# Second layer's matrix scaled by rows on VectorE, the last sums in two banks, an early exponential, and the weighing one slot sooner

## The reference

```python
x = _layernorm(x + L0(x, adj))        # (adj @ x + x) @ W + b, divided by its own length
x = _layernorm(x + L1(x, adj))        # 5 steps of a gated recurrent unit; each multiplies by adj
x = _layernorm(x + L2(x, adj))
x = _layernorm(x + L3(x, adj))

# L2
A_hat = adj + eye
d = sum(A_hat, axis=-1) ** (-0.5)
A_norm = d[:, None] * A_hat * d[None, :]
out = (A_norm @ x) @ W.T + b
# L3
A = softmax(where(adj > 0, e[cumsum(adj > 0) - 1], NEG), axis=1)
out = (A * eye) @ (x @ W0) + (A * (1 - eye)) @ (x @ W1) + bias
```

## Time and profile before

| | |
|---|---|
| median of 3 runs | 771.02 us (769.65 to 773.0) |
| the profiled execution | 769.01 us |
| its span, first to last instruction | 767.1 us |
| busy: PE, DVE, ACT, POOL | 98%, 81%, 67%, 22% |
| granted TensorE clock | 0.998 |
| moved by DMA | 16.60 MB |

### The profile page before, as it was taken

How to read it: one execution, slowest core, us unless ns; L and a number is a source line. 1 busy time by engine, 2 the same in 40 slices (tenths; PEclk the granted TensorE clock), 3 DMA queues, 4 the chain that set the end, 5 groups by cost and what they waited for, 6 DMA issues and landing times.

```text
span 767.1 us, 11992 instructions
## 1 busy us (share of the span) xinstructions
PE 751.2 (98%) x3788; PEld 630.1 (82%) x3788; DVE 624.6 (81%) x1447; ACT 513.7 (67%) x1072; POOL 166.2 (22%) x314
## 2 busy tenths in 40 slices
PE   8999999999999999999999999999999999899996
PEld 7888788888888888888888888888887887789885
DVE  5899998888888788877777777887999998785663
ACT  4799877666667766666666666666587857875444
POOL 1778420000000000000000000000123257764334
PEclk9999999999999999999999999999999999999999
DMA  7500000000030001000000000000000000000112
GB/s 226 204 1 2 1 1 1 1 1 1 0 117 1 1 1 56 1 0 1 1 1 0 0 0 0 0 0 2 1 1 1 1 1 1 3 14 28 56 56 83
DMA packets 9895, 16.60 MB, mean 22 GB/s; under 512 B 2929, under 2 KB 4465, under 8 KB 9201
## 3 DMA queue, kind: packets, MB, share of 16 engines
q1 hardware_dynamic: 9840, 15.94, 6.1%
HBM read 8.59 MB, written 5.24 MB: 18 GB/s over the span
## 4 chain that ended last, share of the span: by engine, by line
PE 78%; DVE 9%; ACT 7%; POOL 2%; issue 2%; DMA 1%; SPq 0%; DVEq 0%; ACTq 0%
PE agg_ps L971 12%; PE agg_ps L973 12%; PE agg_ps L972 12%; PE gate_ps L907 7%; PE gate_ps L909 6%; PE gate_ps L908 6%; PE cand_ps L907 4%; PE cand_ps L909 4%; PE cand_ps L908 4%; PE turn_ps L1010 4%; PE gate_ps L914 2%; PE cand_ps L914 2%; DVE stats L810 2%; ACT res L428 2%; ACT feat L505 1%
## 5 line engine op out<-in xcount | busy, mean ns | idle before, releaser
L971 PE MATMUL agg_ps<-adj_hi,nat_hi 128*128 128x512 f32 x384 | 152.1, 396 | 0.0
L973 PE MATMUL agg_ps<-adj_hi,nat_lo 128*128 128x512 f32 x384 | 150.1, 391 | 0.0
L972 PE MATMUL agg_ps<-adj_lo,nat_hi 128*128 128x512 f32 x384 | 149.6, 390 | 0.0
L629 POOL TENSOR_SCALAR shift<-mean_var 128x4 f32<-128x4 f32 x64 | 25.6, 400 | 427.1 <-DVE mean_var L814 424.8
L767 DVE TENSOR_TENSOR agg_lo<-agg_ps,agg_hi 128x512 fp32r<-128x512 f32 x80 | 55.2, 690 | 65.0 <-ACT agg_hi L457 65.0
L490 ACT ACTIVATE reset_hi<-gate_r 128x512 fp32r<-128x512 f32 x80 | 50.6, 633 | 83.1 <-DVE gate_r L784 83.1
L973 PEld LDWEIGHTS agg_ps<-adj_hi,nat_lo 128*128 128x128 f32 x384 | 72.1, 188 | 16.2
L972 PEld LDWEIGHTS agg_ps<-adj_lo,nat_hi 128*128 128x128 f32 x384 | 72.2, 188 | 15.6
L971 PEld LDWEIGHTS agg_ps<-adj_hi,nat_hi 128*128 128x128 f32 x384 | 72.1, 188 | 15.4 <-DVE adj_lo L833 0.3
L474 ACT ACTIVATE gate_r<-gate_ps,bias 128x512 f32<-128x512 f32 x80 | 55.2, 690 | 43.5 <-PE gate_ps L909 43.5
L457 ACT ACTIVATE agg_hi<-agg_ps 128x512 fp32r<-128x512 f32 x80 | 48.7, 608 | 45.3 <-PE agg_ps L973 45.3
(11 more groups left out here) (181 smaller groups left out, 1794.2 us busy)
## 6 DMA issues: line engine op xcount, KB each, us to landing
res<-in_x SPq DMA_DIRECT2D x16, 256.0 KB, 5.3
out<-res SPq DMA_DIRECT2D x16, 256.0 KB, 2.0
rows<-in_adj SPq DMA_DIRECT2D x4, 256.0 KB, 4.0
adj_hi<-eye_hi SPq DMA_DIRECT2D x1, 1024.0 KB, 9.6
adj_lo<-eye_lo SPq DMA_DIRECT2D x1, 1024.0 KB, 11.5
later<-in_adj SPq DMA_DIRECT2D x1, 1024.0 KB, 6.5
mix_rows<-mix SPq DMA_DIRECT2D x1, 1024.0 KB, 8.0
later<-mix_rows SPq DMA_DIRECT2D x1, 1024.0 KB, 4.9
```

Of the source, the lines that this page charges most:

```text
L971: pe.matmul(ps, nat_hi[:, b, k, :], m_hi[:, k, :], start=(k == 0), stop=False)
L972: pe.matmul(ps, nat_hi[:, b, k, :], m_lo[:, k, :], start=False, stop=False)
L973: last = pe.matmul(ps, nat_lo[:, b, k, :], m_hi[:, k, :], start=False, stop=(k == T - 1))
```

## The change

Four edits are made.

1. L2's matrix is no longer transposed on TensorE. `adj_hi + adj_lo` is the transposed `adj`, so DVE adds the two into `later` and adds the identity to the block's own 128 columns (slots 39 to 42, `WHOLE_AT`), and multiplies each block by `d_cols`, the row of all scales (slots 42 to 45). ACT and DVE make `eye_hi` and `eye_lo` from `later`. The row comes by two DMAs: `row_d` to DRAM, then back spread over all partitions. The four turns "l2", the scaling of rows on ACT and `diag_d` go.
2. For unit 127 the sums lie in two banks, two quarters in each; TensorE reports each half. DVE takes statistics of the first half after the first report. DVE adds the epsilon itself, subtracts the mean while POOL takes the power, and ends with one multiplication of 512 columns. For unit 126, DVE also takes the epsilon and the negated mean from POOL.
3. ACT takes one exponential of one column, `warm`, at the end of slot 100.
4. The reciprocal and the diagonal's multiplication move to the head of DVE's slot 106, and the weighing (ACT and DVE) from slot 107 to the end of slot 106.

```diff
-SCALE_AT = SUM_AT + 3
-L2_AT = SCALE_AT + 3
+WHOLE_AT = SUM_AT + 2
+L2_AT = WHOLE_AT + T
 assert L2_AT + T < LOOP_FROM
 
 EXP_AT = AFTER + 6
 INV_AT = EXP_AT + T
-WEIGH_AT = INV_AT + 1
-MIX_AT = WEIGH_AT + 1
+MIX_AT = INV_AT + 2
...
+        def last_sums():
+
+            one, two = layer_ps[(UNITS - 1) % 4], agg_ps[UNITS % 2]
+            return [ps[:, :].rearrange("p (t d) -> p t d", t=T)[:, part, :] for ps, part in zip((one, two), HALVES)]
...
+            sp.wait_ge(row_d_made, 1)
+            sp.dma_start(d_dram[0].rearrange("(t p) -> p t", p=P), row_d[:, :],
+                         allow_slow_non_contiguous=True).then_inc(d_stored, 16)
+            sp.wait_ge(d_stored, 16)
+            sp.wait_ge(turned, TURN_NO["value", T - 1] + 1)
+            sp.dma_start(d_cols[:, :], d_dram[0:1, :].to_broadcast([P, N])).then_inc(d_cols_in, 16)
             sp.wait_ge(mix_stored, 16)
-            sp.wait_ge(turn_read, reads(TURN_NO["l2", T - 1]))
+            sp.wait_ge(l2_lo_made, T)
...
-                for k in range(2 * (s - SCALE_AT), 2 * (s - SCALE_AT) + 2):
-                    if 0 <= k < T:
-                        act.wait_ge(rows_again, 16)
-                        act.wait_ge(row_d_made, 1)
-                        act.activation(later[:, k, :], later[:, k, :], ACT.Copy,
-                                       scale=row_d[:, k:k + 1]).then_inc(rows_scaled, 1)
                 k = s - L2_AT
                 if 0 <= k < T:
                     act.wait_ge(mix_stored, 16)
-                    n = TURN_NO["l2", k]
-                    act.wait_ge(turned, n + 1)
-                    act.activation(eye_hi[:, k, :], turn_ps[n % 2][:, :], ACT.Copy,
+                    act.wait_ge(l2_scaled, k + 1)
+                    act.activation(eye_hi[:, k, :], later[:, k, :], ACT.Copy,
                                    scale=row_d[:, k:k + 1]).then_inc(l2_hi_made, 1)
+                if s == EXP_AT - 2:
+
+                    act.wait_ge(diag_in, 16)
+                    act.activation(warm[:, :], row_max[:, 0:1], ACT.Exp)
...
-                if s == WEIGH_AT:
+                if s == INV_AT:
...
+                    if n >= UNITS - 2:
+                        pool.wait_ge(eps_added, n - UNITS + 3)
+                        pool.tensor_tensor(rstd[:, i % RING, :], mean_var[:, i % RING, :, 1], half[:, :],
+                                           ALU.pow).then_inc(rstd_made, 1)
+                        if n == UNITS - 2:
+                            pool.wait_ge(mean_negated, 1)
+                            pool.wait_ge(rstd_made, i + 1)
+                            pool.tensor_tensor(shift[:, i % RING, :], shift[:, i % RING, :], rstd[:, i % RING, :],
+                                               ALU.mult).then_inc(shift_made, 1)
+                        continue
...
+            def last_norm(i):
+
+                mean, var = (mean_var[:, i % RING, :, j:j + 1] for j in range(2))
+                for h, (ps, part) in enumerate(zip(last_sums(), HALVES)):
+                    if h == 0:
+                        dve.wait_ge(gate_done, UNITS)
+                    else:
+                        dve.wait_ge(half_done, 1)
+                    for t in range(part.start, part.stop):
+                        last = dve.bn_stats(stats[:, i % 4, t, :], ps[:, t - part.start, :])
+                last.then_inc(statted, 1)
+                dve.wait_ge(statted, i + 1)
+                for t in range(T):
+                    last = dve.bn_aggr(mean_var[:, i % RING, t, :], stats[:, i % 4, t, :])
+                last.then_inc(aggregated, 1)
+                dve.wait_ge(aggregated, i + 1)
+                dve.tensor_scalar(var, var, EPS_LN, None, ALU.add).then_inc(eps_added, 1)
+                for ps, part in zip(last_sums(), HALVES):
+                    link(dve.tensor_tensor(res[:, B - 1, part, :], ps, mean[:, part, :].to_broadcast([P, T // 2, D]),
+                                           ALU.subtract))
+                dve.wait_ge(rstd_made, i + 1)
+                dve.tensor_tensor(res[:, B - 1, :, :], res[:, B - 1, :, :],
+                                  rstd[:, i % RING, :, None].to_broadcast([P, T, D]), ALU.mult).then_inc(last_normed, 1)
...
+                if s == INV_AT:
+                    dve.wait_ge(exp_made, T)
+                    link(dve.reciprocal(exp_inv[:, :], exp_sum[:, :]))
+                    dve.wait_ge(diag_exp_made, T)
+                    dve.tensor_tensor(diag[:, :], diag[:, :], exp_inv[:, :], ALU.mult).then_inc(exp_inv_made, 1)
...
+                    if s == UNITS - 1:
+
+                        dve.wait_ge(agg_hi_made, s)
+                        for ps, part in zip(last_sums(), HALVES):
+                            last = dve.tensor_tensor(ps, res[:, B - 1, part, :],
+                                                     bias_rows[:, c:c + 1, :].to_broadcast([P, T // 2, D]), ALU.add)
+                        last.then_inc(seeded, 1)
...
+                    if n == UNITS - 2:
+                        mean, var = (mean_var[:, i % RING, :, j] for j in range(2))
+                        dve.wait_ge(aggregated, i + 1)
+                        dve.tensor_scalar(var, var, EPS_LN, None, ALU.add).then_inc(eps_added, 1)
+                        dve.tensor_scalar(shift[:, i % RING, :], mean, -1.0, None, ALU.mult).then_inc(mean_negated, 1)
...
-                if s == SCALE_AT:
-                    dve.wait_ge(row_d_made, 1)
-                    dve.wait_ge(turned, TURN_NO["value", T - 1] + 1)
-                    for t in range(T):
-                        last = dve.tensor_scalar(diag_d[:, t * P:(t + 1) * P], ident[:, :], row_d[:, t:t + 1], None, ALU.mult)
-                    last.then_inc(diag_d_made, 1)
+                k = s - WHOLE_AT
+                if 0 <= k < T:
+                    own = slice(k * P, (k + 1) * P)
+                    dve.wait_ge(row_sum_made, T)
+                    dve.tensor_tensor(later[:, k, :], adj_hi[:, k, :].bitcast(F32), adj_lo[:, k, :].bitcast(F32),
+                                      ALU.add).then_inc(l2_whole, 1)
+                    dve.wait_ge(l2_whole, 2 * k + 1)
+                    dve.tensor_tensor(later[:, k, own], later[:, k, own], ident[:, :], ALU.add).then_inc(l2_whole, 1)
                 k = s - L2_AT
                 if 0 <= k < T:
                     dve.wait_ge(l2_hi_made, k + 1)
-                    dve.scalar_tensor_tensor(out=eye_lo[:, k, :], in0=turn_ps[TURN_NO["l2", k] % 2][:, :],
+                    dve.scalar_tensor_tensor(out=eye_lo[:, k, :], in0=later[:, k, :],
                                              scalar=row_d[:, k:k + 1], in1=eye_hi[:, k, :].bitcast(F32), op0=ALU.mult,
-                                             op1=ALU.subtract).then_inc(turn_read, 1)
+                                             op1=ALU.subtract).then_inc(l2_lo_made, 1)
+                k = s - L2_AT + 1
+                if 0 <= k < T:
+                    dve.wait_ge(d_cols_in, 16)
+                    dve.wait_ge(l2_whole, 2 * k + 2)
+                    dve.tensor_tensor(later[:, k, :], later[:, k, :], d_cols[:, :], ALU.mult).then_inc(l2_scaled, 1)
...
-                    dve.wait_ge(exp_made, T)
-                    link(dve.reciprocal(exp_inv[:, :], exp_sum[:, :]))
-                    dve.wait_ge(diag_exp_made, T)
-                    dve.tensor_tensor(diag[:, :], diag[:, :], exp_inv[:, :], ALU.mult).then_inc(exp_inv_made, 1)
-                if s == WEIGH_AT:
...
+                if u == UNITS - 1:
+
+                    pe.wait_ge(turn_read, reads(TURN_NO["back", u - B]))
+                    halves = layer_ps[u % 4], agg_ps[(u + 1) % 2]
+                    for m, at in ((feat[:, B - 1, :], W_SELF), (agg_all[:, u % 2, :], W_L3)):
+                        if at == W_L3:
+                            pe.wait_ge(agg_hi_made, u + 1)
+                        for h, half_ps in enumerate(halves):
+                            for t in range(HALVES[h].start, HALVES[h].stop):
+                                cols = slice(t * P, (t + 1) * P)
+                                last = pe.matmul(half_ps[:, cols], m[:, cols], w_all[:, at, :], start=False,
+                                                 stop=at == W_L3, skip_group_check=True)
+                            if at == W_L3:
+                                last.then_inc((gate_done, half_done)[h], 1)
+                    return
...
-                    elif kind == "l2":
-                        pe.wait_ge(rows_scaled, T)
-                        pe.wait_ge(diag_d_made, 1)
-                        for t in range(T):
-                            cols = slice(t * P, (t + 1) * P)
-                            last = pe.transpose(to[:, cols], later[:, t, i:i + T * (P - 1) + 1:T], ident[:, :])
-                            if t == i:
-                                last = pe.matmul(to[:, cols], ident[:, :], diag_d[:, cols], start=False, stop=True,
-                                                 skip_group_check=True)
```

(32 more changed lines are left out.)

8 lines of the change are left out of this document (3 added, 5 removed).

## The result

The changed kernel takes 767.16 us in the median of 20 executions (765.05 to 769.09); the kernel before, measured beside it, 769.26 us. The ratio is 0.9963, with a 95% interval of 0.9955 to 0.9971. By the ratio that is 2.85 us faster (2.2 to 3.5), by the medians 2.1 us, where the forecast was 4.4 us. The interval excludes no change, but 0.37% is less than the 0.5% that the prediction took as the least that such a measurement can tell. The profiled execution took 765.98 us, its span is 763.6 us, 3.5 less than before's 767.1.

A forecast was written before the change was run, and what follows sets the result against it. The prediction took TensorE, busy 98% of the span, as the bound. Gains of 2.8 + 0.4 + 1.2 = 4.4 us from 771.02 gave 766.6 us, range 764.2 to 769.2.

The forecast's parts named there:

- Edit 1, TensorE: Slots 43 to 46: without transposes and diagonal products, four slots take 26.41 us instead of 29.18, a gain of 2.8 us.
- Edit 1, DVE: Slots 39 to 45: added work makes DVE about 1.1 us late at most; no TensorE stall, upper bound 0.5 us.
- The two DMAs: Row of scales to DRAM and back: d_cols there at about 246.5, needed about 257.3, eleven us spare.
- Edit 3: Early exponential: TensorE's 1.9 us wait at slot 103 becomes about 1.2 at slot 101, a lead of 0.7 us.
- the rival that rested on it: Early table load: it costs the drain too, or a second load is made; 1.4 us less gain, 768.0; chance 0.05.
- Edit 4: Slots 106 to 109: first softmax turn 1.5 to 2 us sooner, then a wait of about 2 us for line 833.
- the term of 0.4 us: L3's matrix: gain of early exponential and earlier weighing together, 0.4 us, with ends -1.5 and 2.5.
- Edits 3 and 4, the clock: L3's matrix, slots 101 to 109: waits were priced in us only; no term for a change of clock, size none.
- Edit 2: End of the kernel: DVE ends 1.5 us sooner, 0.3 taken off for the stores, net 1.2 us (0.4 to 1.6).
- the sign of colliding stores: End of the kernel: more than 2.7 us from DVE's last instruction to the end would mean the stores collide.
- Outside the span: Execution time beyond the profiled span: 1.9 us, taken to stay outside all edits.
- the chain wins: Slot 106: DVE's wait passes through POOL and ACT; early exponential and earlier weighing lose about 1 us, 768.0; chance 0.17.

The follow-up runs named there:

- rows_alone: Kernel before with only L2's matrix made by a row of scales instead of transposes on TensorE: 766.45 us, ratio 0.9961 to the kernel before.
- table_weigh: Kernel before with only the early exponential and the weighing one slot sooner: 770.83 us, ratio 1.0018 to the kernel before.
- table_alone: Kernel before with only the early exponential at the end of slot 100: 768.49 us, ratio 0.9985 to the kernel before.
- weigh_alone: Kernel before with only the weighing moved into the reciprocal's slot: 770.92 us, ratio 1.0006 to the kernel before.
- end_alone: Kernel before with only the last sums in two banks and the shorter last norm: 768.30 us, ratio 0.9992 to the kernel before.
- mix_first: Changed kernel with ACT's copy adj_hi of L3's matrix moved ahead of its slot's norms: 765.61 us, ratio 0.9944 to the kernel before.
- rows_and_end: Kernel before with L2's row of scales and the shorter end, without early exponential or earlier weighing: 765.58 us, ratio 0.9952 to the kernel before.
- after_again: The changed kernel itself, unaltered, run and profiled a second time: 767.27 us, ratio 0.9975 to the kernel before.
- filled_wait: Changed kernel with nine useless matmuls ahead of slot 109's turn "back": 766.05 us, ratio 0.9953 to the kernel before.
- filled_both: Changed kernel with nine useless matmuls ahead of slot 109's turn "back" and four ahead of slot 0: 765.94 us, ratio 0.9959 to the kernel before.
- both_moves: Changed kernel with adj_hi ahead of its slot's norms and the early exponential behind slot 100's aggregate copy: 763.97 us, ratio 0.9935 to the kernel before.

## Why the prediction was right and wrong

The median lies inside the range, 0.6 us above the forecast in absolute time, but that nearness is luck. The forecast started from 771.02 us, the median of three executions of the kernel before, which took 769.26 in 20: 1.8 us too high. The gain was 2.1 us by the medians (2.85 by the ratio) where 4.4 were forecast. The two errors nearly cancel. Point by point:

- **Edit 1, TensorE: right.** From slot 39 to 47 DVE's line 824 goes from 0.71 us later than before to 2.07 us earlier: 2.78 us, forecast 2.8. (The 0.7 us stem from the start, where the first product came 0.63 us later; in the profiles of all kernels it came at 10.08 to 11.14 us, with the landing of the first loads.) Alone it gives 3.0 us by its ratio.
- **Edit 1, DVE: the slot was costed too high.** 6.8 us were forecast for slots 43 to 45, 6.50 measured. No wait, as taken.
- **The two DMAs: right.** In the trace of after, the spread load is issued at 242.01 and such a load takes 4.9 us, so `d_cols` is there at 246.9; it is used at 259.19. 12 us to spare, forecast 11.
- **Edit 3: near.** 1.2 us were forecast for the wait at slot 101; 0.9 with the other edits, 1.17 alone. The load took 1.28 us and the exponential began 1.29 after it, with no time for the drain that the Trainium skill ("ScalarE: Activation LUTs", "What ACT_TABLE_LOAD costs") puts at 1.38 us; the rival that rested on it did not come.
- **Edit 4: the mechanism was right, what it costs was not.** The 2.25 us for line 898 were foreseen (about 2), a wait of 0.6 us at slot 107 was not. The prediction put POOL's start 0.1 to 0.45 us later and ACT's norm 1.0 us sooner to 0.5 later, and took a gain of 0.4 us. Against rows_alone POOL started 0.58 us later, the norm 0.39 later, and the turn 0.41 later: DVE's lateness was passed on in part, and the term of 0.4 us had the wrong sign. The kernel before alone hides this. Against its profile the turn came 2.26 us earlier, which is 2.07 from the slots and 0.19 more; but the 0.19 is 0.60 from the smaller wait at slot 103, which rows_alone has too, less 0.41.
- **Edits 3 and 4, the clock: missing.** The other step that failed: an idle time was priced as its length alone. Three small waits that became one long one are about equal in sum (3.9 and 3.7 us), but behind the long one the granted clock fell in the profiled execution of table_weigh, and by the groups of times in many others, at 1.6 us each. By their ratio edits 3 and 4 cost 1.4 us where they should have gained 0.4: 1.8 us, as much as the shortfall in the gain or a little less (1.55 by the ratio, 2.3 by the medians).
- **Edit 2: right in the span.** DVE ended 3.87 us sooner, 2.26 of it from before: 1.61, forecast 1.5. From there to the end it was 2.77 us instead of 2.4, forecast 0.3 more, measured 0.37; just past the 2.7 that I had named as the sign of colliding stores; no run tells whether the stores are the cause. Net 1.24, forecast 1.2.
- **Outside the span: wrong.** "1.9 more than its span, which stays outside all edits": it was 1.81 to 1.93 us in every execution of before, of table_alone, of weigh_alone and of table_weigh, 2.05 to 2.12 in rows_alone, 2.13 to 2.21 in end_alone, and 2.1 to 2.6 with both. Edits 1 and 2 cost 0.2 to 0.3 us each there. What of them does it (new semaphores, in edit 1 also an array in DRAM) was not taken apart.

The sum, in the trace: 2.78 + 0.19 + 1.24 = 4.2 us, less 0.7 of a later start, is the 3.5 us between the spans. Between the shorter executions of both kernels the medians differ by 769.2 - 765.8 = 3.4 us; the 0.5 us lost outside the span is already off this. The rest, 767.16 instead of 765.8, is put down to the low stretches. Of the rivals, "the chain wins" named the right loser, edits 3 and 4 at -1.0 us. Lateness passed on, its cause, is 0.4 us of it in the trace.

Left open: why the wait at slot 103 is 1.9 us in the profiles of the kernel before and of weigh_alone and 1.23 to 1.28 in three others with the same code there; why the clock fell in some executions and not in others behind a wait of the same length (2.25 us in both profiles of the changed kernel without a fall, 2.24 in table_weigh with one), and where the long executions of mix_first and of weigh_alone have theirs, beyond the one at the start that a profile caught.

## What to carry to other kernels

Do not add up an engine's idle time: see where it is collected. Moving work so that several short waits of TensorE become one long one can cost time beyond the waits themselves, and one profiled execution may show nothing of it; look at every execution's time and granted clock, and where times come in groups, find the group's stretch in a profile. When a step is moved, look for the copy that stands behind someone else's wait in an in-order queue: the 2.25 us here lay in ACT's queue, not in the work. And compare with a kernel that has the other edits of the same stretch, not only with the kernel before: against the kernel before, edits 3 and 4 seemed to gain 0.2 us, against rows_alone they lose 0.4.

## What the runs showed of the hardware

- In three profiles TensorE's granted clock went from 1.00 to 0.50 (2.4 to 1.2 GHz) while it stood idle or within 1 us behind it, and came back by itself after 3.4 us: behind 2.24 us of idle time (table_weigh), 1.77 (weigh_alone) and 1.79 (rows_and_end). Behind 1.64 and 2.25 us (the kernel after), 2.25 (after_again), 1.73 (filled_wait), 1.72 (end_alone), 1.89 (weigh_alone, slot 103) and 1.9 us (before) it stayed at 1.00. So the length of the idle time alone does not decide it.
- With matmuls that compute nothing of use in the idle time, long executions were rare: 1 of 11 in filled_wait and filled_both, against 18 of 31 in the changed kernel. All 10 executions that also had the start filled, with zeros for operands, had a mean clock of 0.998 or more; rows_alone (none of five long) and both_moves (one of six) did nearly as well without any filling, so the part of the start is not shown.
- ACT's table load fitted into a wait of its own queue at no cost: the norm behind it began at 631.85 us in both_moves, and at 631.91 in the kernel after, where it stood ahead of the load.
